# Shared and routed experts of one layer on one core: the first routed tiles' transposes and first product put among the shared expert's last products

## The reference

```
scores  = sigmoid(h @ gate_w);  combine[t, e] = weight of expert e for row t, 4 of 32 experts
up      = einsum('th,ehi->tei', h, Wu);   act = relu(up)**2
routed  = einsum('tei,te,eih->th', act, combine, Wd)
shared  = relu(h @ Wsu)**2 @ Wsd
out     = routed + shared
```

## Time and profile before

| what | value |
|---|---|
| median of 3 runs | 1200.43 us (1200.29 to 1203.81) |
| profiled execution, its own time | 1198.15 us |
| span of the profile, first to last instruction | 1196.2 us |
| mean granted TensorE clock | 0.972 |
| PE busy | 1073.0 us, 90% of the span |
| VectorE, ScalarE, GpSimd busy | 48%, 46%, 36% |
| stage 4 with its seam | from about 772 us to about 1160 us of the span |

### The profile page before, as it was taken

One profiled execution on the slowest core, in us unless ns is written; L12 is line 12 of the kernel. 1 busy time (PEld: TensorE's weight loads), 2 busy tenths in 40 slices (PEclk: granted clock), 3 DMA queues, 4 the chain that ended last, 5 costly groups with the idle time before them and its releaser, 6 DMA issues.

```text
span 1196.2 us, 17242 instructions
## 1 busy us (share of the span) xinstructions
PE 1073.0 (90%) x4892; PEld 846.3 (71%) x4893; DVE 577.2 (48%) x1114; ACT 546.7 (46%) x896; POOL 427.9 (36%) x331
## 2 busy tenths in 40 slices
PE   1989989999999999999979999979899988998950
PEld 0547768888788788878868888867677766776740
DVE  6976747814834380400538953034444444444423
ACT  4643526334332433333523343357666656666640
POOL 1012303211320322122432342246576665676630
PEclk9899999999999999999989999989999999999985
DMA  9504285526324523242832250057989989888769
GB/s 288 206 1 176 79 309 176 170 86 220 131 98 160 182 96 103 108 158 88 294 146 106 86 170 36 1 142 156 293 196 228 242 233 253 233 140 196 151 127 374
DMA packets 96913, 198.46 MB, mean 166 GB/s; under 512 B 11616, under 2 KB 31072, under 8 KB 96352
## 3 DMA queue, kind: packets, MB, share of 16 engines
q1 hardware_dynamic: 76464, 147.43, 35.3%
q0 software_dynamic: 18816, 45.43, 19.4%
q10 hardware_dynamic: 1584, 4.98, 1.2%
HBM read 137.78 MB, written 60.03 MB: 165 GB/s over the span
## 4 chain that ended last, share of the span: by engine, by line
PE 66%; DMA 12%; issue 7%; DVE 6%; POOL 5%; ACT 2%; SPq 1%; POOLq 0%; ACTq 0%; DVEq 0%
PE bank L600 31%; PE bank L916 21%; DMA xg<-h_d,idc 6%; PE bank L517 4%; PE bank L1485 4%; DMA last<-shx_d 2%; DMA wd<-in_L_ffn_Wd 2%; PE bank L1477 2%; POOL xg L1624 1%; POOL res_d L1646 1%; DMA res_d<-yo,idy 1%; POOL shx_d L1646 1%; PE bank L924 1%; POOL idc L1655 1%; ACT yo L1557 1%
## 5 line engine op out<-in xcount | busy, mean ns | idle before, releaser
L897 POOL TENSOR_TENSOR ksp_lo<-ra,ksp_hi 128x512 fp32r<-128x512 f32 x96 | 146.4, 1525 | 471.0 <-ACT ksp_hi L846 471.0
L1485 PE MATMUL bank<-wu,xT 128*128 x672 | 163.8, 387 | 17.8 <-issue 10.7
L916 PE MATMUL bank<-vring,ksp_hi 128*128 128x512 f32 x512 | 159.4, 393 | 0.0
L1485 PEld LDWEIGHTS bank<-wu,xT 128*128 128x128 f32 x672 | 122.0, 192 | 38.7 <-issue 25.3
L600 PE MATMUL bank<-wds,aT 128*128 128x512 f32 x504 | 138.3, 410 | 2.1 <-DVE aT L1595 1.5
L839 ACT ACTIVATE ra<-bank 128x512 f32<-128x512 f32 x96 | 57.4, 597 | 173.9 <-PE bank L600 170.4
L1600 DVE TENSOR_TENSOR wds<-wd,wds 128x1024 fp32r<-128x1024 f32 x84 | 103.0, 1227 | 35.3 <-issue 35.2
L846 ACT ACTIVATE ksp_hi<-ra 128x512 fp32r<-128x512 f32 x96 | 60.7, 632 | 124.9 <-PE bank L916 124.3
L1624 POOL DMA_INDIRECT xg<-h_d,idc x84 | 96.2, 1145 | 38.5 <-issue 26.6
L916 PEld LDWEIGHTS bank<-vring,ksp_hi 128*128 128x128 f32 x512 | 95.5, 188 | 20.1
L600 PEld LDWEIGHTS bank<-wds,aT 128*128 128x128 f32 x504 | 89.1, 190 | 19.5 <-DVE aT L1595 1.9
(11 more groups left out here) (258 smaller groups left out, 1892.1 us busy)
## 6 DMA issues: line engine op xcount, KB each, us to landing
vring<-wcv_d SPq DMA_DIRECT2D x64, 512.0 KB, 3.3
wu<-in_L_ffn_Wu SPq DMA_DIRECT2D x32, 512.0 KB
wd<-in_L_ffn_Wd SPq DMA_DIRECT2D x32, 512.0 KB
hT_d<-hT SPq DMA_DIRECT2D x16, 512.0 KB, 3.5
hTb<-hT_d SPq DMA_DIRECT2D x4, 2048.0 KB, 9.4
raw_wcv<-in_L_attn_Wcv SPq DMA_DIRECT2D x4, 1024.0 KB, 6.9
raw_wck<-in_L_attn_Wck SPq DMA_DIRECT2D x4, 1024.0 KB, 9.5
f<-in_L_attn_x SPq DMA_DIRECT2D x4, 1024.0 KB, 7.0
```

The lines of the kernel that those rows point to most:

```text
L897: nc.gpsimd.tensor_tensor(ksp[1][:, i % 2], ra[:, i % 2], ksp[0][:, i % 2], ALU.subtract).then_inc(sem("klo_in"), 1)
L916: m = nc.tensor.matmul(bank[j][:], ksp[l][:, i % 2, j * P:(j + 1) * P], rhs(r), start=i == 0 and k == 0, stop=i == last and k == 2)
L1485: m = nc.tensor.matmul(bank[2 + u][:, 0:EI], xT4[:, u, c * P:(c + 1) * P], slot_of(wu4[:, :, c * EI:(c + 1) * EI], e), start=c == 0, stop= ...
```

## The change

Tin(0) moves ahead of down(6) of the last shared block, up(0) and tin(1) move between down(6) and down(7), and turn(0) stands behind down(7). PE's single wait for all of `sh_in` ahead of tin(0) becomes two: one copy of `so` ahead of turn(0), all of them ahead of the loop. A wait for `rows_in` (VectorE has read bank 6) and one for `kc_free` (ScalarE has emptied the last up product's bank) are new. ScalarE's last block ends without the four copies of `so`; they come behind `w_hi`, `x_in(0)`, `relu(0)` and `x_in(1)` of stage 4, and in the order of banks 2, 3, 0, 1. ScalarE no longer waits for the end of the last down product before it enters stage 4. For all this the banks of stage 4 are dealt anew (tin 6 and 7, up 4 and 5, turn 2 and 3, down 0 and 1), and `yo` and `wds` change places in SBUF. GpSimd's, VectorE's and SyncE's programs keep their order.

```diff
-        yo = at("yo", [P, YRING, H], F, 14)
-        wds = at("wds", [P, 2, 2, EI // P * H], R, 34)
+        yo = at("yo", [P, YRING, H], F, 77)
+        wds = at("wds", [P, 2, 2, EI // P * H], R, 14)
...
                 if i == BETWEEN_AT and between:
                     between(pe)
+            if b == NB - 1:
+                return down
             down(NSI - 2)
             down(NSI - 1)
...
-        def act_block3(act, b, router=False):
+        def act_block3(act, b, router=False, last=False):
...
+            if not last:
+                act_rows3(act, b, router)
+
+        def act_rows3(act, b, router=False):
             act.wait_ge(sem("vc_done"), 2 + N3 + (b + 1) * NSI)
             act.wait_ge(sem("bs_st"), 16 * b + 16)
-            for j in range(BT):
+            for j in (2, 3, 0, 1):
                 nc.scalar.activation(so[:, j], bank[j][:], ACT.Copy).then_inc(sem("sh_in"), 1)
...
-            pe.wait_ge(sem("sh_in"), NB * BT)
             pe.wait_ge(sem("owner_in"), 1)
             passes = passes_of(pe)
+            pe.wait_ge(sem("rows_in"), 1)
             tin(0, 0, 0)
+            down3(NSI - 2)
+            pe.wait_ge(sem("kc_free"), N4 + 2)
             up(0, 0, first_owners(pe, 1)[0])
             tin(0, 1, 1)
+            down3(NSI - 1)
+            pe.wait_ge(sem("sh_in"), (NB - 1) * BT + 1)
             turn(0, 0)
+            pe.wait_ge(sem("sh_in"), NB * BT)
             with pe.Fori(0, PASSES - 1) as i, pe.If(i < passes):
...
-            act.wait_ge(sem("vc_done"), 2 + N4)
             act.wait_ge(sem("owner_in"), 1)
...
             x_in(1, 1)
+            act_rows3(act, NB - 1)
             for t in range(1, YRING + 1):
```

More of the change, by code:

```diff
@@ L1128, in stage3_tensor @@
             pe_block3(pe, 2, between=lambda pe: pe_ids(pe, (0, 1)))
-            pe_block3(pe, 3, between=lambda pe: pe_ids(pe, (2, 3)))
+            return pe_block3(pe, 3, between=lambda pe: pe_ids(pe, (2, 3)))
         ORDER3 = (("u", 0), ("u", 1), ("d", 0), ("d", 1), ("u", 2), ("d", 2), ("u", 3), ("d", 3))
@@ L1170, in stage3_scalar @@
             act_block3(act, 0, router=True)
-            with act.Fori(1, NB) as b:
+            with act.Fori(1, NB - 1) as b:
                 act_block3(act, b)
+            act_block3(act, NB - 1, last=True)
         def pool_numbers(pool):
@@ L1469, in slot_of, with stage4_tensor @@
             return ring[:, bass.ds(e & 3, 1)].rearrange("p a n -> p (a n)")
-        def stage4_tensor(pe):
+        def stage4_tensor(pe, down3):
             def tin(i, t, u):
@@ L1476, in tin @@
                 for c in range(C):
-                    m = nc.tensor.transpose(bank[u][:, c * P:(c + 1) * P], xg[s][:, c * P:(c + 1) * P], ident[:])
+                    m = nc.tensor.transpose(bank[6 + u][:, c * P:(c + 1) * P], xg[s][:, c * P:(c + 1) * P], ident[:])
                 m.then_inc(sem("t4"), 1)
@@ L1484, in up @@
                 for c in range(C):
-                    m = nc.tensor.matmul(bank[2 + u][:, 0:EI], xT4[:, u, c * P:(c + 1) * P],
+                    m = nc.tensor.matmul(bank[4 + u][:, 0:EI], xT4[:, u, c * P:(c + 1) * P],
                                          slot_of(wu4[:, :, c * EI:(c + 1) * EI], e), start=c == 0, stop=c == C - 1)
@@ L1492, in turn @@
                 for c in range(EI // P):
-                    m = nc.tensor.transpose(bank[4 + u][:, c * P:(c + 1) * P], a4[:, u, c * P:(c + 1) * P], ident[:])
+                    m = nc.tensor.transpose(bank[2 + u][:, c * P:(c + 1) * P], a4[:, u, c * P:(c + 1) * P], ident[:])
                 m.then_inc(sem("at4"), 1)
@@ L1499, in down @@
                 pe.wait_ge(sem("y4"), g + 1)
-                split_product(bank[6 + u][:], lambda s, c: aT4[:, u, s, c * P:(c + 1) * P],
+                split_product(bank[u][:], lambda s, c: aT4[:, u, s, c * P:(c + 1) * P],
                               lambda s, c: wds[:, u, s, c * H:(c + 1) * H], EI // P).then_inc(sem("d4"), 1)
@@ L1533, in x_in @@
                 act.wait_ge(sem("u4"), g + 1)
-                nc.scalar.activation(xT4[:, u], bank[u][:], ACT.Copy).then_inc(sem("xt4"), 1)
+                nc.scalar.activation(xT4[:, u], bank[6 + u][:], ACT.Copy).then_inc(sem("xt4"), 1)
             def relu(g, u):
@@ L1538, in relu @@
                 act.wait_ge(sem("at4"), g + 1)
-                nc.scalar.activation(a4[:, u], bank[2 + u][:, 0:EI], ACT.Relu).then_inc(sem("r4"), 1)
+                nc.scalar.activation(a4[:, u], bank[4 + u][:, 0:EI], ACT.Relu).then_inc(sem("r4"), 1)
             def a_hi(g, u):
@@ L1543, in a_hi @@
                 act.wait_ge(sem("d4"), g + 1)
-                nc.scalar.activation(aT4[:, u, 0], bank[4 + u][:, 0:EI], ACT.Copy).then_inc(sem("ah4"), 1)
+                nc.scalar.activation(aT4[:, u, 0], bank[2 + u][:, 0:EI], ACT.Copy).then_inc(sem("ah4"), 1)
             def w_hi(g, u, e):
@@ L1594, in a_lo @@
                 dve.wait_ge(sem("ah4"), g + 1)
-                nc.vector.tensor_tensor(aT4[:, u, 1], bank[4 + u][:, 0:EI], aT4[:, u, 0],
+                nc.vector.tensor_tensor(aT4[:, u, 1], bank[2 + u][:, 0:EI], aT4[:, u, 0],
                                         ALU.subtract).then_inc(sem("al4"), 1)
@@ L1770, in _ @@
             stage2_tensor(pe)
-            stage3_tensor(pe)
-            stage4_tensor(pe)
+            down3 = stage3_tensor(pe)
+            stage4_tensor(pe, down3)
 def kernel(**inputs):
```

2 lines of the change are left out of this document (1 added, 1 removed).

## The result

The changed kernel takes 1203.78 us, the median of 20 runs, beside 1199.97 us for 20 runs of the kernel before. The ratio is 1.0040 with a 95% interval of 1.0024 to 1.0057: 4.8 us slower (2.9 to 6.8). The two medians by themselves lie 3.8 us apart. The forecast was 4.9 us slower, and a time of 1205.3 us. The profiled execution took 1201.53 us, its span is 1199.7 us, 3.5 us more than before.

A forecast was written before the change was run, and what follows sets the result against it. PE was taken as two thirds of the chain of waits, stage 4's gathers and scatters the rest. PE's terms put up(1) 3.6 us later, GpSimd's queue the first scatter 4.9 later: 1205.3 us, range 1201.0 to 1208.8.

The forecast's parts named there:

- The wait that moves: PE ahead of tin(0) and down(6): stands 7.0 us from 772.40 until tile 0's gathered rows land at 779.4.
- an edit which the prediction put at nothing: ScalarE's missing vc_done wait ahead of w_hi: it and VectorE's w_lo run early, at no cost.
- The clock after the wait: PE after tile 0 lands: clock at half for 2.8 to 6.3 us of work, costing 1.4 to 3.15, taken as 2.2 us.
- The register load ahead of up(0): PE ahead of up(0): a register load costs 0.24 us, between nothing and 1.27.
- The copies and the loop's entry: Behind down(7): four copies end at 792.06, PE's loop entry needs 1.3 us, up(1) at 793.36, 3.6 us later.
- The sum for GpSimd: GpSimd's queue at the loop's start: fetch 4 at 798.37, 1.79 us to the first scatter at 800.16, 4.9 us later.
- PE at tile 6: In the loop: GpSimd's delayed fetch 6 holds PE, tin(6) at 813.1, where PE by itself would be at 810.4.
- From there to the end: Rest of the loop behind tile 6: all runs 4.9 us late.
- The rivals: Three other outcomes: part given back (chance 0.17), rows there in time (0.08), more lost (0.13).
- The rows are there in time: Rival at the seam: no wait at 772.40, 4.3 us gained through GpSimd, time 1196.2; chance 0.08.
- Part of it is given back: Rival in the loop: gathers land sooner, leaving a loss near 2.1 us, time 1202.5; chance 0.17.
- more is lost: Rival: clock half for 6.3 us, landing and load at high ends, tile 4 or 6 late; 8.4 us, 1208.8; chance 0.13.

The follow-up runs named there:

- e2: Changed kernel with ScalarE's first split of expert weights behind its copy of tile 0 instead of ahead; +4.0 us (+1.3 to +6.5) against the kernel before.
- e4: e3 without the wait for copies ahead of tin(0); ScalarE makes the copies first and splits weights behind x_in(0); -1.6 us (-4.1 to +1.0) against the kernel before.
- e1: Changed kernel with GpSimd's gathers of tiles 0 and 1 behind ksp_lo of slice 5 instead of 7; -2.3 us (-4.7 to +0.2) against the kernel before.
- e3: Changed kernel with only PE's order put back: down(6), down(7), tin(0), up(0), tin(1), turn(0); +3.1 us (+0.4 to +5.9) against the kernel before.
- e6: e1 plus 16 unread identity transposes on PE between turn(0) and the wait for the copies; -3.6 us (-6.1 to -1.0) against the kernel before.
- e9: Changed kernel plus 60 unread identity transposes ahead of tin(0) and 16 behind turn(0); +4.7 us (+2.4 to +7.1) against the kernel before.
- e5: e1 with up(0) behind down(7), copies in two pairs around tile 0's relu, all-copies wait at stage 4's first down; -5.0 us (-7.2 to -2.8) against the kernel before.
- e7: Kernel before with the changed kernel's banks, buffers, copy order and two new waits, PE's and ScalarE's order kept; -1.3 us (-4.1 to +1.4) against the kernel before.
- e8: Changed kernel with the wait for all copies moved from the loop's entry to stage 4's first down product; +6.6 us (+4.1 to +9.1) against the kernel before.
- e10: e5 plus 8 identity transposes ahead of turn(0) and 6 behind it; 1191.63 us, ratio 0.9939, -7.3 us (-10.1 to -4.4) against the kernel before.

## Why the prediction was right, step by step

- **The wait that moves: right in place, too small in size.** Forecast 7.0 us ahead of tin(0), measured 7.93. The gather was issued when the rows said, but 0.9 us slower. That is from an edit which the prediction put at nothing: ScalarE's missing wait lets VectorE's subtraction run beside that issue (e2). Without it tile 0 lands where the prediction said (e4: 779.45, forecast 779.4).
- **The clock after the wait**: 2.2 us forecast. Tin(0) and down(6) took 4.87 us (780.41 to 785.28) instead of 0.36 + 2.72: 1.8 us.
- **The register load ahead of up(0)**: 0.24 forecast, nothing measured here; in e1, where PE reaches it without a wait before, 0.47.
- **The copies and the loop's entry**: copies done at 792.45 (forecast 792.06); entry 1.76 us (792.45 to 794.21) instead of 1.3. It took 1.74 to 1.79 us in the changed kernel, e1, e2, e3, e6 and e9, whose loop entry waits for the copies, and 1.26 to 1.32 behind turn(0) in the kernel before, e4, e5, e7 and e8, where nothing holds it there. Up(1) at 794.21, forecast 793.36.
- **Missed: the second fall of the clock.** The prediction counted the gap behind down(7) but not what it does to the clock. Up(1) took 3.65 instead of 1.89 us and the scaled result of tile 0 was 6.1 us late, not 3.6. E6 and e9 show that it is the idle time that does it.
- **The sum for GpSimd: its end is 1.2 us too small, and another path came last.** Fetch 4 at 799.23 (forecast 798.37): 0.39 for the later copies, and 0.47 because it came 6.78 us behind their end and not 6.31. Scatter at 801.36 (forecast 800.16). The prediction had GpSimd's queue set the scatter; in the changed kernel PE's result did, 1.53 us behind the scaling as before the change, and the queue alone would by estimate have let it go at 801.02 (799.23, fetch 4's 1.49 us and the 0.30 that stand between two issues). The 1.79 us from fetch to scatter, which the prediction took from tile 1, is too much for the queue alone: in e6, e8 and e9 it is 1.25. So the 4.9 rests on a path that did not bind, and that it came near the measured time is luck in part. The queue was close behind, though: in e8, where PE was 3 us quicker, the scatter was only 0.8 us sooner and no gain can be seen in the time.
- **PE at tile 6**: forecast 813.1, measured 814.05.
- **From there to the end**: forecast that nothing is given back. In the pair of profiles 2.6 us of 6.1 are missing at the end, but e7 shows the same steps without any change of the order at the seam, and the table's agreement of scatter and time says that it holds in the mean. The scatter is 6.1 us late and the time 4.8 us longer (2.9 to 6.8); what lies between them is within the noise. That the forecast of 4.9 hit the middle is in part luck: a path that is 1.2 us longer than forecast met an interval 4 us wide.
- **The rivals.** "The rows are there in time" was made true in e1: the sign turned at the scatter, but by 1.8 us and not the 4.3 worked out, for the second fall of the clock; the time, -2.3 us (-4.7 to +0.2), is not separated from nothing. "Part of it is given back" (2.1 us) and "more is lost" (8.4 us) both lie outside the measured interval.

Not settled: whether the new banks save a part in stage 4, as e7's profile would allow; and whether the 0.9 us of the slower issue would show in a time once the clock no longer hides it, which wasn't tried.

## What to carry to other kernels

Before an instruction is moved ahead of others on an in-order engine, read from the trace when its last input lands, by the chain of the engine that issues it, and not from the fact that it never waited where it stood: here it had only never been asked early enough. Move the producer with it: with the gathers two slices sooner the same PE order lost nothing against the kernel before (e1), and with up(0) behind down(7), the copies in two pairs and no wait at the loop's entry as well (e5) it was 5 us faster; with the gaps filled (e10) 7 us, though these two are not separated. And when one engine's step is made earlier, look at what else its follower queues behind: of PE's 3 us only 0.8 reached the scatter while GpSimd's queue stood behind the store of the copies (e8).

## What the runs showed of the hardware that was not expected

- TensorE's clock fell in a stretch without a long gap: in e4 the longest gap in the 8 us before was 1.45 us and up(1) still took 3.09 us. In e5 the gaps before were 0.98 and 1.32 us, and up(1) took 3.19; with 14 transposes put into these two gaps (e10) it took 1.99.
- An idle wait of PE could be filled without delaying what it waited for: 60 transposes took 6.71 us and ended 1.34 us before the wait did, and tin(0) started no later (7.1 us behind `ksp_lo` in both kernels).
- An indirect gather's issue on GpSimd took 2.1 us instead of 1.2 when a VectorE subtraction of 128x1024 ran beside it, in four kernels of four. Fetch 4 was longer by 0.54, 0.82 and 0.94 us where the subtraction had begun first and overlapped it by 0.67, 0.95 and 1.07 us (changed kernel, e1, e5), and not at all where the issue began first (e8).
- PE's entry of the loop took 1.74 to 1.79 us from the end of the last copy to the first product where it waited there for the copies (six kernels), and 1.26 to 1.32 us behind turn(0) where nothing held it (five kernels).
